# A recurrent layer and a mixture of experts on one core: the gates spread by DMA, the gate product two units behind

## What is computed

```python
xw = jnp.einsum('ntd,dh->nth', x, Wx) + b
next_h = jnp.tanh(xw_t + prev_h @ Wh)             # 32 steps
xn = xf * rsqrt(mean(xf * xf) + EPS) * norm_scale # 1024 tokens
logits = xn @ wg + bg
vals, idx = jax.lax.top_k(logits, K)              # 4 of 16
gates = softmax(vals)                             # scattered to gate_full[t, e]
h = einsum('th,ehd->etd', xn, w1) + b1
a = minimum(h[..., ::2], 7);  b = clip(h[..., 1::2], -7, 7)
s = a * sigmoid(1.702 * a) * (b + 1.0)
y = einsum('eti,eih->eth', s, w2) + b2
t = einsum('eth,te->th', y, gate_full)
out = x + (xf + t)
```

## Time and profile before

| | us |
|---|---|
| median of 3 runs | 128.18 (126.57 to 128.47) |
| the profiled execution | 127.02 |
| its span | 124.7 |
| PE busy | 111.3 (89%) |
| DVE busy | 89.8 (72%) |
| ACT busy | 65.4 (52%) |
| POOL busy | 24.0 (19%) |

### The profile page before, as it was taken

One profiled execution on the slowest core, in us unless ns is written; L12 is line 12 of the kernel. 1 busy time (PEld: TensorE's weight loads), 2 busy tenths in 40 slices (PEclk: granted clock), 3 DMA queues, 4 the chain that ended last, 5 costly groups with the idle time before them and its releaser, 6 DMA issues. The chain is left out here.

```text
span 124.7 us, 1891 instructions
## 1 busy us (share of the span) xinstructions
PE 111.3 (89%) x611; PEld 91.6 (73%) x611; DVE 89.8 (72%) x238; ACT 65.4 (52%) x141; POOL 24.0 (19%) x44
## 2 busy tenths in 40 slices
PE   3669989979999999999999399999999999999850
PEld 2558779969989999899988398877766776677310
DVE  0105659899748999769977779897678877887830
ACT  4014593657663567566756166644665466546210
POOL 5200212940004066206401513000000000000000
PEclk9999999999999999999999999999999999999999
DMA  2899900000000000000000010000001000000003
GB/s 59 178 324 323 334 27 5 0 0 3 0 3 0 5 0 0 0 0 5 0 0 0 3 42 5 0 0 0 0 13 29 0 0 0 8 0 0 0 0 84
DMA packets 6189, 4.52 MB, mean 36 GB/s; under 512 B 754, under 2 KB 6100, under 8 KB 6148
## 3 DMA queue, kind: packets, MB, share of 16 engines
q1 hardware_dynamic: 6148, 4.34, 12.3%
q0 software_dynamic: 32, 0.07, 0.2%
HBM read 3.88 MB, written 0.52 MB: 35 GB/s over the span
## 5 line engine op out<-in xcount | busy, mean ns | idle before, releaser
L458 ACT ACTIVATE relu_a<-psA,lim_b1a 128x256 f32<-128x256 f32 (+1 forms) x48 | 25.8, 546 | 30.4 <-PE psA L808 30.4
L685 DVE TENSOR_SCALAR lin<-psB,one_b1b 128x256 f32<-128x256 f32 (+1 forms) x48 | 26.0, 569 | 16.5 <-PE psB L808 16.2
L838 PE MATMUL psY<-actg,w_sb 128*128 128x256 f32 (+1 forms) x96 | 33.6, 459 | 0.4 <-DVE actg L703 0.3
L808 PE MATMUL psA<-xn_hi,w_hi 128*128 128x256 f32 (+1 forms) x48 | 23.7, 495 | 0.0
L466 ACT ACTIVATE swish<-relu_a,limit_col 128x512 f32<-128x512 f32 x32 | 23.1, 722 | 1.0
L716 DVE SCALAR_TENSOR_TENSOR act<-lin,swish 128x512 f32<-128x512 f32 x32 | 22.3, 695 | 0.0
L703 DVE TENSOR_TENSOR actg<-act,psG 128x512 f32<-128x512 f32 x31 | 21.0, 678 | 0.0
L838 PEld LDWEIGHTS psY<-actg,w_sb 128*128 128x128 f32 x96 | 16.9, 189 | 4.1 <-DVE actg L703 1.9
L808 PE MATMUL psB<-xn_hi,w_hi 128*128 128x256 f32 (+1 forms) x48 | 16.7, 347 | 0.0
L808 PE MATMUL psA<-xn_hi,w_lo 128*128 128x256 f32 (+1 forms) x48 | 15.8, 330 | 0.0
L808 PE MATMUL psA<-xn_lo,w_hi 128*128 128x256 f32 (+1 forms) x48 | 15.8, 330 | 0.0
(11 more groups left out here) (105 smaller groups left out, 131.4 us busy)
## 6 DMA issues: line engine op xcount, KB each, us to landing
w_sb<-in_L_ffn_w SPq DMA_DIRECT2D x4, 512.0 KB, 6.7
w_sb<-in_L_ffn_w SPq DMA_DIRECT2D x4, 256.0 KB, 7.2
x_sb<-in_x SPq DMA_DIRECT2D x1, 448.0 KB, 4.7
out<-y_sb SPq DMA_DIRECT2D x8, 32.0 KB, 1.6
out<-y_sb SPq DMA_DIRECT2D x4, 64.0 KB, 1.7
x_sb<-in_x SPq DMA_DIRECT2D x1, 64.0 KB, 2.1
wh_sb<-in_L_cond_Wh POOLq DMA_DIRECT2D x1, 64.0 KB, 2.4
wx_sb<-in_L_cond_Wx SPq DMA_DIRECT2D x1, 64.0 KB, 2.2
```

Source lines behind the costliest of these rows:

```text
L458: last = nc.scalar.activation(relu_a[:, u % 2, o], psA[u % 2][:, o], ACT.Relu, scale=-1.0, bias=lim_b1a[:, e0 + k:e0 + k + 1])
L685: last = nc.vector.tensor_scalar(lin[:, v % 2, o], psB[v % 2][:, o], one_b1b[:, e0 + k:e0 + k + 1], LIMIT + 1.0, ALU.add, ALU.min)
L808: last = nc.tensor.matmul(o, w[:, e0 + k, a, :], x_part[:, cols(c)], start=(m == 0), stop=(m == 2))
L838: last = nc.tensor.matmul(psY[:, 0:n], w2_sb[:, e0 + k, :], actg[:, u % SUM_DEPTH, part(c, k)], start=False, stop=(e0 + k == E - 1))
```

## The change

- The select matmuls and psG are gone. Gates are transposed into a new bank psX (the former psG), copied by ACT to `gT` (16 partitions, fp32), written by DMA to a DRAM scratch `gate_rows`, and read back from there by four transfers for each pair of tiles, each 4 experts x 256 tokens to all 128 partitions (`gate_cols`). The gate product reads `gate_cols` from SBUF.
- The gate product runs two units behind (`GATE_LAG = 2`), down four (`LAG = 4`); `act` has 6 buffers.
- ACT's relu and gelu write in place into psA, and DVE's act reads psA. Up A(v) now waits for act(v - 2).
- b2 is multiplied in fp32 and the rounded parts of gates and b2 are gone. Chunk 2 accumulates in psR. Finished rows use psX; psM and psX have an order each.
- Head: the warm matmuls are 6 of 512 columns, then single ones of 256 between the steps. x comes in three pieces (64, 192, 256 KB), Wh through SP, b and norm_scale through ACT's queue, all of w1 before w2. The transposes of tiles 4 to 7 lie around x_wx and in unit 0; the last 6 rounding operations of w1 on ACT follow units 0 to 2. POOL rounds the second half of w1 for all pairs.

```diff
-    WARM, WARM_START = 128, 9
-    LAG = 2
+    WARM, WARM_START, WARM_GAP = 512, 6, 256
+    LAG = 4
+    GATE_LAG = 2
+    ACT_DEPTH, SUM_DEPTH = 6, 5
...
-    RSTD, GATES, GATES_T = [[None] + [v + k for v in STATS[1:]] for k in (1, 3, 4)]
-    ROWS_OUT = [UNIT0[c + 1] + LAG + 3 for c in range(NC - 1)] + [None]
+    RSTD = [None] + [v + 1 for v in STATS[1:]]
+    GATES, GATES_T = [[k] + [v + 3 + k for v in STATS[1:]] for k in (0, 1)]
+    ROWS_OUT = [UNIT0[c + 1] + LAG + 2 for c in range(NC - 1)] + [None]
...
+            def spread_gates(q):
+
+                qc = slice(q * PW, (q + 1) * PW)
+                sp.wait_ge(x_read, psX_turn(("gates", q)))
+                sp.dma_start(gate_rows[:, qc], gT[:, qc]).then_inc(rows_written, 16)
+                sp.wait_ge(rows_written, 16 * (q + 1))
+                if GATE_HALF[q] in GATE_HALF[:q]:
+                    sp.wait_ge(actg_done, UNIT0[1])
+                for k in range(GATE_GROUPS):
+                    es = slice(k * EQ, (k + 1) * EQ)
+                    sp.dma_start(gate_cols[:, es, gate_slice(q)],
+                                 gate_rows[es, qc].partition_broadcast(P)).then_inc(cols_loaded[q][k], 16)
...
+            for q in range(3):
+                spread_gates(q)
+            sp.wait_ge(x_read, psX_turn(("out", 0)))
+            store_rows(0)
+            spread_gates(3)
...
-                    last = nc.scalar.activation(relu_a[:, u % 2, o], psA[u % 2][:, o], ACT.Relu, scale=-1.0,
+                    last = nc.scalar.activation(psA[u % 2][:, o], psA[u % 2][:, o], ACT.Relu, scale=-1.0,
...
-                nc.scalar.activation(swish[:, u % 3, 0:w], relu_a[:, u % 2, 0:w], ACT.Gelu_apprx_sigmoid, scale=-1.0,
+                nc.scalar.activation(psA[u % 2][:, 0:w], psA[u % 2][:, 0:w], ACT.Gelu_apprx_sigmoid, scale=-1.0,
...
+            def gate_product(u):
+
+                dve.wait_ge(act_done, u + 1)
+                gates_here(dve, u)
+                if u >= SUM_DEPTH:
+                    dve.wait_ge(y_mm, u - SUM_DEPTH + 1)
+                r = unit(u)[2]
+                for o in pieces(u):
+                    n = o.stop - o.start
+                    last = nc.vector.tensor_tensor(actg[:, u % SUM_DEPTH, o].rearrange("p (r n) -> p r n", r=r),
+                                                   act[:, u % ACT_DEPTH, o].rearrange("p (r n) -> p r n", r=r),
+                                                   gate_block(u, o).rearrange("p (r n) -> p r n", r=r) if r == 1
+                                                   else gate_block(u, o), ALU.mult)
+                    last.then_inc(actg_done, 1)
...
-                nc.tensor.matmul(psY[:, 0:n], b2_rows[:, :], gT[:, cols(c)], start=True, stop=False)
+                nc.tensor.matmul(bank[:, 0:n], b2_sb[:, :], gT[:, cols(c)], start=True, stop=False)
...
                     if v >= 2:
-                        pe.wait_ge(relu_done, v - 1)
+                        pe.wait_ge(act_done, v - 1)
                     up(v, 0, psA[v % 2], a_mm)
...
-                if 1 <= v <= NU:
-                    lay_gates(v - 1)
```

More of the change, by code:

```diff
@@ L273, in psM_turn, with psX_turn @@
                 g = pair_group(q)
-                later += [(STATS[q], 1, ("stats", g)), (RSTD[q], 2, ("rstd", g)), (GATES_T[q], 3, ("gates", q))]
-            later += [(ROWS_OUT[c], 4, ("out", c)) for c in range(NC - 1)]
+                later += [(STATS[q], 1, ("stats", g)), (RSTD[q], 2, ("rstd", g))]
             order += [k[2] for k in sorted(later, key=lambda k: k[:2])]
+            return order.index(what) + 1
+        def psX_turn(what):
+            later = [(GATES_T[q], 1, ("gates", q)) for q in range(NQ)]
+            later += [(ROWS_OUT[c], 2, ("out", c)) for c in range(NC - 1)]
+            order = ["x"] + [k[2] for k in sorted(later, key=lambda k: k[:2])]
             return order.index(what) + 1
@@ L725, in _ @@
                     gates_scale(q)
-                    gates_high(q)
+            for u in range(NU - GATE_LAG, NU):
+                gate_product(u)
             dve.wait_ge(y_mm, NU)
@@ L809, in up @@
                 last.then_inc(done, 1)
-            def lay_gates(u):
-                c, e0, r = unit(u)
-                n = CHUNKS[c] * P
-                if u == UNIT0[c]:
-                    pe.wait_ge(m_read, psM_turn(("gates", first_pair(c + 1) - 1)))
-                if u == NU - 1:
-                    pe.wait_ge(m_read, psM_turn(("out", NC - 2)))
-                elif u >= 1:
-                    pe.wait_ge(actg_done, u)
-                for k in range(r):
-                    last = nc.tensor.matmul(gate_bank(u)[:, k * n:(k + 1) * n], select[:, e0 + k, :], gT[:, cols(c)],
-                                            start=True, stop=True)
-                last.then_inc(g_mm, 1)
             def down(u):
@@ L837, in down @@
                 for k in range(r):
-                    last = nc.tensor.matmul(psY[:, 0:n], w2_sb[:, e0 + k, :], actg[:, u % SUM_DEPTH, part(c, k)],
+                    last = nc.tensor.matmul(bank[:, 0:n], w2_sb[:, e0 + k, :], actg[:, u % SUM_DEPTH, part(c, k)],
                                             start=False, stop=(e0 + k == E - 1))
@@ L887, in _ @@
             raw_logits(pair_tiles(0), psB[0]).then_inc(raw_mm, 1)
-            for j in range(4, NT):
-                if j == X_SPLIT:
-                    lay_rstd(1)
-                last = transpose_x(j, psG, j - 4)
-            last.then_inc(x_t, 1)
+            pe.wait_ge(x_loaded, 16)
+            transpose_x(4, psX, 0)
+            lay_rstd(1)
             x_wx(2, XW_TILES - 2)
+            transpose_x(5, psX, 1)
             for v in range(NU + LAG):
```

312 lines of the change are left out of this document (149 added, 163 removed).

## The result

| | before | after |
|---|---|---|
| median | 128.1 us (126.55 to 128.49) | 143.68 us (6 runs, 142.84 to 149.47) |
| ratio | | 1.126, 95% interval 1.115 to 1.136 |
| profiled execution | 127.02 us, span 124.7 | 149.47 us, span 147.4 |
| forecast | | 124.3 us, 118.5 to 129.0 |

The change makes the kernel 12.6% slower, and the forecast was wrong in sign and size. The profiled execution of after is the slowest of its six (the others' spans are 140.8 to 144.5); its places are those of all, its sizes a few us above the median.

The account below looks back on a forecast made before the run. PE was taken to set the pace, DVE about 0.5 us behind. 35.8 + 81.2 - 6.2 - 2.1 + 1.3 + 1.0 + 0.7 = 111.7; + 4.9 + 5.25 = 121.85 us span, giving 124.3 us, range 118.5 to 129.

Parts of the forecast that it names:

- The head: Start of the kernel: step(1) at about 6.65 us, step(7) at 14.5, up(0) at 19.65, up(1) at 24.4.
- Selects off PE: Units 3 to 29 on PE: 27 selects of 0.23 us fall away, 6.2 us gained.
- out(0)'s wait: PE's wait for psM at out(0)'s transpose, behind normalise: gone with psX, 2.1 us gained.
- DVE pacing units 13 to 17: From lin(13) to lin(18) DVE sets the pace instead of PE: 1.0 us lost, 0.5 to 1.5.
- Activation in PSUM: DVE's act reads psA: +0.05 us a unit (0 to 0.15), hidden; up A(v+2) waiting for act(v) costs nothing.
- The end: Behind the last up B: last down ends 4.9 us later instead of 4.18, then 5.25 us as before.
- the sum: All terms together: up(4) at 35.8, last up B at 111.7, span 121.85 us, median 124.3 us.
- the term: Gates' broadcast from DRAM: first piece 3.6 us (2.2 to 4.9), later 1.6 each; up(4) at 35.8 instead of 34.11.
- the 0.7 us (0 to 2) that the sum had for pair 3: Chunk 2: gate_product(16) gets its gates late, so up(20) starts 0.7 us later.
- the rival: Slow broadcast, all partitions reading the same rows, chance 0.25: half rate 128 us (0.15), a third or less 133 us (0.10).
- The clock rival: The head reaches 2.4 GHz, shortening step periods and units 0 and 1: over 6 us, 119 us in all; chance 0.22.

Follow-up runs that it names:

- experiment 10: The kernel before with the transposes of out(0) and out(1) one unit later in PE's order: 124.78 us, ratio 0.977.
- kernel 8: The changed kernel with the contiguous scratch (the four rows of a piece adjacent) and nothing else, stores where the change has them: 124.7 us.
- kernels 6 and 7: Changed kernel, stores of chunk 0 behind the fourth spread; 6: rows of a piece adjacent, 126.23 us; 7: 1 KB padding, rows 5 KB apart, 126.35 us.
- kernel 2: The changed kernel with the four reads of each pair taking their 512 KB from w1 in DRAM, every partition its own rows: 128.16 us.
- experiment 3: The changed kernel with the last pair's write and reads issued ahead of the store of chunk 0: 140.52 us.
- experiment 9: The changed kernel with 21 and 58 unread 512-column matmuls on PE ahead of up A(4) and up A(20), transfers still slow: 138.3 us.
- kernel 12: As kernel 11, with the lag worked off at units 21 and 25, so the last units are two and four behind: 120.87 us, ratio 0.944.
- kernel 11: The changed kernel with contiguous scratch, stores behind the fourth spread, GATE_LAG 4 instead of 2 and LAG 6 instead of 4: 121.33 us, ratio 0.946.

## Why the forecast was wrong, step by step

**Right.** The head: step(1) at 6.68 (6.65 forecast), step(7) at 13.60 (14.5), up(0) at 18.80 (19.65), up(1) at 23.36 (24.4); the last three about a microsecond early, since six step periods took 6.92 us and not 7.9: I had charged all seven keep_warm matmuls, and part of them must lie in gaps that are there anyway (argued, not tried). gates_scale started at 26.99 and was done at 27.71 (28.2), the write landed at 30.03 (30.8). Selects off PE: the unit is 2.25 us, as worked out from 2.49 - 0.23. out(0)'s wait: gone; experiment 10 alone gave 2.2 for my 2.1. DVE pacing units 13 to 17: PE waits 0.42 us for act at unit 16, and 0.47 at unit 12, for my 1.0. Activation in PSUM: act takes 677 ns against 695 before, ACT's second pass 662 against 722, so the +0.05 a unit had the wrong sign. The end: 137.40 to 147.4, 10.0 us for my 4.9 + 5.25. With fast transfers the sum holds: kernel 8 has up(4) at 36.13 (35.8), the last up B issued at 112.63 (111.7), span 122.7 (121.85), 124.7 us (124.3). That it holds so closely is in part luck. Its first piece takes 4.4 us for my 3.6, which the early head makes good, and its clock never fell; kernels 6 and 7, with the same fast reads, came to 126.2 and 126.4.

**Wrong, the term.** "3.6 us, bounds 2.2 and 4.9" for the first piece, "1.6 us each" for the later ones. Measured: 5.8 us (30.03 to 35.85), and some 3.4 us each behind it (landings at 35.7, 39.2, 42.8 and 45.8), 155 GB/s. So up(4) started at 37.29 and not at 35.8, and the 0.7 us (0 to 2) that the sum had for pair 3 became a wait of 13.16. Both bounds came from loads whose partitions read different rows; w1's rows are of 1 KB too, and 128 KB apart. None tested rows that lie 4 KB apart and are shared by all partitions. I had named the sharing as a risk. Kernel 6 clears it as a cause by itself; it takes the distance of 4 KB as well, which I overlooked. With own rows the first piece took 3.3 us (kernel 2), with shared rows next to each other 4.2 to 4.4 (kernels 6 and 8): 3.6 was about right for the bytes. The write landed 1.4 us after its issue, for my 1.8. The fixed 2.0 us that the prediction quotes from the Trainium skill (DMA: Bandwidth & Descriptors, section Anatomy of one DMA) stand there for transfers that GpSimd issues; these come from SP, and the measured 1.4 decides.

**Wrong, the rival.** "At half the load rate ... 128 us, no change", "decides the sign from about 2.5 times on". The rate was half, and it cost not 4 us over the forecast but 19. I priced only how much later each first piece lands. Three things were missing. Four pieces of 3.4 us and more are a burst of about 16 us; pair 2's burst (79.37 to 95.8) is still under way when pair 3's write and reads are due, and the write, which I priced at 1.8 us in every place, took 7.6. Next, the stores between them took 6.51 us to issue; by experiment 3 they add little over 1 us, since the write waits for the burst with or without them. Together they make 14.16 us of DVE's wait out of a step that the rival priced at 3.2 or less. Last, I took a wait to cost its own length; behind these waits the clock stayed at 1.2 GHz, 5.4 us by experiment 9.

**The clock rival** was wrong in this profile: the head's matmuls keep the 0.21 us distance.

## What to carry to other kernels

A DMA price taken from another transfer holds for the same source pattern only: look at which rows the partitions share and how far apart they lie. Here shared rows 4 KB apart were slow, and the same rows adjacent or 5 KB apart were not; own rows 128 KB apart were fast as they were. When a transfer may be slower than assumed, follow its whole burst through the queues (the next small write, the stores, the next burst), not just its first piece. And count a wait of TensorE of 2 us and more as its length plus what the half-rate clock behind it may cost, 0 to 4.6 us in these profiles; where the data can come earlier or be used later, as with a longer lag, both go.

## What had not been expected of the hardware

- 512 KB read from four 1 KB rows 4 KB apart, shared by 128 partitions: about 155 GB/s. Shared rows 5 KB apart or adjacent: 337 GB/s. Own rows for each partition, 128 KB apart: 322. Neither the sharing nor such a distance is slow alone.
- A 16 KB write lands after 1.4 us with the engines free, and after 7.6 to 10.0 behind such a burst, from SP's queue as from ACT's, within 1.5 us of the burst's last read; even the issue of four stores then takes 6.51 us instead of 1.77.
- Behind a wait of 2 to 5 us TensorE's clock falls for very different times: not at all behind 2.82 us, for 3.5 us behind 4.11, for some 10 us behind 2.46. What decides it stayed open.
- In some executions of the new head the clock is up between about 5 and 8 us. The profile of kernel 12 is one (others are read from their mean clock of 0.92 and their short span alone); PE's timeline and the granted clock there, then kernel 11's:

```profile
5.65 0.49 PE L809 MATMUL psA<-warm 128*128 128x256 bf16 x3
...
9.00:12.00 3.00, 3.00 (x19) 2.69 (x17) 0.41 (x3) 1.50 (x6) 1.30 (x2) 0.50 0.76 202
```
```profile
6.06 0.83 PE L804 MATMUL psA<-warm 128*128 128x256 bf16 x3
...
9.00:12.00 3.00, 3.00 (x17) 2.78 (x17) 0.26 (x2) 1.32 (x6) 0.73 (x1) 1.00 0.77 215
```

Three matmuls of 256 columns span 0.49 us in the one and 0.83 in the other, and up(0) starts at 17.44 instead of 18.80. From 9 us on both run at 1.2 GHz, yet the granted clock reads 0.50 in the first and 1.00 in the second. So a granted clock of 1.00 early in a kernel does not mean 2.4 GHz; the distance of the matmuls tells. A part of the clock rival thus does occur, worth 1.4 us and not 6; what decides it stayed open too.
